# Loads of the next tile in mid-turn of the MLP loop, and a gather ring of 16 slots in the second graph layer

## What is computed

```python
xn = _layernorm(x)
h   = relu(sage_conv(xn, src, dst, W1l, b1, W1r))       # layer 1
gnn = sage_conv(h, src, dst, W2l, b2, W2r)              # layer 2
x = x + gnn + mix(xn)                                   # linear attention, layer norm, MLP, layer norm
x = x + ffn(_layernorm(x))                              # 8 experts, hidden 1024, top 1
# sage_conv: agg = segment_sum(x[src], dst); mean = agg / max(count, 1); mean @ Wl.T + bl + x @ Wr.T
```

## Time and profile before

| what | value |
|---|---|
| time, median of 3 runs | 2454.78 us (2453.99 to 2458.47) |
| the profiled execution: its own time | 2453.61 us |
| its span in the profile | 2451.8 us |
| PE busy | 1925.4 us (79%) |
| DVE busy | 1148.8 us (47%) |
| ACT busy | 549.0 us (22%) |
| POOL busy | 1702.3 us (69%) |
| mean granted clock of PE | 0.891 |

### The profile page before, as it was taken

How to read it: one execution, slowest core, us unless ns; L and a number is a source line. 1 busy time by engine, 2 the same in 40 slices (tenths; PEclk the granted TensorE clock), 3 DMA queues, 4 the chain that set the end, 5 groups by cost and what they waited for, 6 DMA issues and landing times.

```text
span 2451.8 us, 45561 instructions
## 1 busy us (share of the span) xinstructions
PE 1925.4 (79%) x9589; PEld 1190.2 (49%) x9590; DVE 1148.8 (47%) x3201; ACT 549.0 (22%) x1242; POOL 1702.3 (69%) x1773
## 2 busy tenths in 40 slices
PE   3799988878688887776899999877665543679998
PEld 2455555544455555543455555444332211368886
DVE  8544443433577777764555545433332221242221
ACT  6444333333222222221222222111100000101110
POOL 6777777777777777757777777777777777164442
PEclk9999999898899999997899999988776665689999
DMA  7444444444444444434454555444443333245551
GB/s 219 132 124 126 124 123 121 122 118 118 132 135 137 133 133 137 132 97 149 146 166 151 164 157 164 147 153 142 138 141 116 114 116 105 89 141 167 168 167 63
DMA packets 155000, 332.67 MB, mean 136 GB/s; under 512 B 34853, under 2 KB 89095, under 8 KB 154917
## 3 DMA queue, kind: packets, MB, share of 16 engines
q0 software_dynamic: 85824, 248.21, 34.6%
q10 hardware_dynamic: 42630, 58.35, 6.9%
q1 hardware_dynamic: 26466, 25.33, 3.4%
HBM read 273.97 MB, written 58.72 MB: 136 GB/s over the span
## 4 chain that ended last, share of the span: by engine, by line
PE 36%; POOL 33%; issue 15%; DVE 7%; DMA 4%; DVEq 2%; POOLq 2%; ACT 1%; ACTq 1%; SPq 0%
POOL big L699 32%; PE bank L538 12%; PE bank L1728 8%; PE bank L1496 6%; PE bank L1716 2%; PE bank L1502 2%; DMA mbuf<-qT_d 1%; PE bank L1526 1%; PE bank L1651 1%; PE bank L1521 1%; DMA big<-hh_d,edges 1%; POOL big L709 1%; POOLq L696 1%; DMA big<-xh_d,edges 1%; POOLq L694 1%
## 5 line engine op out<-in xcount | busy, mean ns | idle before, releaser
L699 POOL DMA_INDIRECT big<-xh_d,edges x782 | 769.8, 984 | 240.5 <-issue 232.4
L699 POOL DMA_INDIRECT big<-hh_d,edges x782 | 752.4, 962 | 261.1 <-issue 227.2
L1496 PE MATMUL bank<-big,S 128*128 x1960 | 589.0, 427 | 245.8 <-SPq L604 218.4
L898 DVE SCALAR_TENSOR_TENSOR S<-edges,tv,iota 128x512 f16<-128x512 f16 x490 | 368.6, 754 | 450.5 <-PE bank L1496 267.6
L1496 PEld LDWEIGHTS bank<-big,S 128*128 128x128 f16 x1960 | 203.7, 104 | 533.6 <-issue 389.8
L1494 PE MATMUL bank<-ones,S 128*128 128x1 f16 x980 | 165.4, 169 | 73.7 <-SPq L604 63.6
L538 PE MATMUL bank<-turned,x1T 128*128 128x512 f32 x392 | 195.6, 622 | 0.0
L720 POOL DMA_INDIRECT out_dram<-big,node_s x56 | 56.8, 1014 | 145.1 <-DVE big L1231 141.2
L1494 PEld LDWEIGHTS bank<-ones,S 128*128 128x128 f16 x980 | 95.5, 97 | 89.5 <-SPq L604 75.7
L1424 ACT ACTIVATE x1T<-bank 128x256 f32<-128x256 f32 x49 | 18.8, 383 | 531.7 <-PE bank L1502 531.7
L1231 DVE SCALAR_TENSOR_TENSOR big<-bank,prob_s,res 128x256 f32<-128x256 f32 x56 | 27.1, 484 | 179.4 <-PE bank L1730 179.4
(11 more groups left out here) (228 smaller groups left out, 2910.4 us busy)
## 6 DMA issues: line engine op xcount, KB each, us to landing
hx_d<-mbuf ACTq DMA_DIRECT2D x49, 512.0 KB
big<-xh_d,edges POOLq DMA_INDIRECT x782
big<-hh_d,edges POOLq DMA_INDIRECT x782
big<-in_fwd_dram SPq DMA_DIRECT2D x8, 1024.0 KB, 6.4
qT_d<-abuf ACTq DMA_DIRECT2D x49, 128.0 KB
hh_d<-HL ACTq DMA_DIRECT2D x49, 128.0 KB
mbuf<-qT_d ACTq DMA_DIRECT2D x49, 128.0 KB, 2.6
hx_d<-res ACTq DMA_DIRECT2D x49, 128.0 KB
```

Of the source, the lines that this page charges most:

```text
L699: e.indirect_dma_start(G[:, r, n % SC, :], None, table, bass.IndirectOffsetOnAxis(ap=srcx[:, n:n + 1], axis=0)).then_inc(d_g[r], 16)
L898: VI.done(e.scalar_tensor_tensor(S[:, walk.u, :, :], dst[:, bass.ds(c * SC, SC)].unsqueeze(2).to_broadcast([P, SC, P]), tv[:, bass.ds(k, 1 ...
L1496: ins = e.matmul(AGG[:], S[:, walk.u, j, :], G[:, bass.ds(slot, 1), j, :].rearrange("p a c -> p (a c)"), start=False, stop=False, skip_gro ...
```

## The change

Three things are changed.

- In `turn_b` on ACT, `next_loads(i)` stands behind the two `x1T` and ahead of the first `finish1` piece and the Gelus. It was the last thing of the turn.
- In layer 2 the ring has 16 slots instead of eight. They lie from the start of `big`, over `xnT` and half of the old ring. POOL's wait for superchunk c names superchunk c-16. Slots that hold no edges are cleared by two memsets of POOL ahead of the first gather of layer 2, behind a wait for ACT's last read of `xnT`; PE waits for the memsets once.
- Because the new ring lies where the experts' weights go, all eight loads of them are issued by SP behind the last sum of layer 2. The bias `fbd_f` is staged in `late`, and SP's wait for it is gone.

The rest is bookkeeping: the semaphores `d_g` of the eight new slots serve as `d_rb` in the experts' stage, with a base that is added to the counts.

```diff
-RING = 8
+RING, RING2 = 8, 16
+RINGS = RING, RING2
...
+        G2 = big[:, 0:RING2 * SC * C].bitcast(F16).rearrange("p (r j c) -> p r j c", r=RING2, j=SC)
+        GS = G, G2
...
-        fbd_f, fbd_t = big[0:3, 0:NE * C], w2r[0:3].rearrange("p h c -> p (h c)").bitcast(BF16)
+        fbd_f, fbd_t = late[0:3, 0:NE * C], w2r[0:3].rearrange("p h c -> p (h c)").bitcast(BF16)
...
-            EVERY = SUPER // NE // PACK * PACK
-            SOON = XN // (HJ * C)
-
-            def expert_rows(k):
+            for c in range(SUPER):
+                relay(1, c)
+            e.wait_ge(s_sum, NS + 2 * ITEMS)
+            for k in range(NE):
                 e.dma_start(wd[:, k:k + 1, :, :].rearrange("p a j c -> p (a j) c"),
                             w["fwd"][k:k + 1].rearrange("a (j p) c -> p (a j) c", p=P)).then_inc(d_wd, 16)
-            for c in range(SUPER):
-                relay(1, c)
-                k, left = divmod(c + 1, EVERY)
-                if left == 0 and k <= SOON:
-                    if k == 1:
-                        e.wait_ge(s_fbd, 1)
-                    expert_rows(k - 1)
-            e.wait_ge(s_sum, NS + 2 * ITEMS)
-            for k in range(SOON, NE):
-                expert_rows(k)
...
                 else:
+                    AX1.wait(e, "xT", TILES - 1)
+                    for c in range(2):
+                        e.memset(G2[:, ring(1, c), len(chunks(c)):, :].bitcast(F32), 0.0).then_inc(p_setup, 1)
                     e.wait_ge(d_h, 3 * OPENED + 16 * TILES)
...
-                        e.wait_ge(s_sum, held + (c + NS + 1 - RING + layer * ITEMS))
+                        e.wait_ge(s_sum, held + (c + NS + 1 - RINGS[layer] + layer * ITEMS))
...
+                if stage < 2:
+                    next_loads(i)
+                elif stage == 2:
+                    with e.If(i.base < TILES - 1):
+                        next_loads(i)
                 if stage <= 2:
                     walk = Ends(e, raw(i), 1, ITEMS_B, TILES * ITEMS_A)
                     finishes(walk, 1)
...
                 if stage <= 2:
                     finishes(walk, ITEMS_B - 1)
-                if stage < 2:
-                    next_loads(i)
-                elif stage == 2:
-                    with e.If(i.base < TILES - 1):
-                        next_loads(i)
...
-                slot = within(e, walk.c % RING, RING - 1)
+                slot = within(e, walk.c % RINGS[layer], RINGS[layer] - 1)
...
+            e.wait_ge(p_setup, 3 + 8 + 2)
...
-                e.wait_ge(d_rb[u], turn * 16 + 16)
+                e.wait_ge(d_rb[u], turn * 16 + (16 + RB_BASE[u]))
```

More of the change, by code:

```diff
@@ L194, in build @@
         G = ringf.bitcast(F16).rearrange("p (r j c) -> p r j c", r=RING, j=SC)
-        assert XN + (RING - PACK) * SC * C >= WD
+        G2 = big[:, 0:RING2 * SC * C].bitcast(F16).rearrange("p (r j c) -> p r j c", r=RING2, j=SC)
+        GS = G, G2
+        assert XN + (RING - PACK) * SC * C >= max(WD, RING2 * SC * C) and NE * C <= PACK * SC * C
         S = sb("S", [P, NS, SC, P], F16)
@@ L341, in build, with chunks, ring @@
         FR = B7
+        def chunks(c):
+            first = (SUPER - 1 - c) * SC
+            return range(min(first, CHUNKS), min(first + SC, CHUNKS))
+        def ring(layer, c):
+            return (layer * SUPER + 1 + c) % RINGS[layer]
         d_x = [sem(n) for n in ("d_x0_w", "d_x1_w2", "d_x2_wd", "d_x3", "d_x4", "d_x5", "d_x6")]
@@ L346, in build @@
         X_IN = 16 * GROUP
-        d_g = [sem(f"d_g{r}") for r in range(RING)]
+        d_g = [sem(f"d_g{r}") for r in range(RING2)]
         d_edges, d_bias, d_ck, s_gb2, d_fbd = (sem(n) for n in ("d_edges", "d_bias", "d_ck", "s_gb2", "d_fbd"))
@@ L415, in build @@
         s_perm, s_fbd = sem("s_perm"), sem("s_fbd")
-        d_rb = [sem(f"d_rb{u}") for u in range(RB_SLOTS)]
+        assert RING2 - RING == RB_SLOTS
+        d_rb = d_g[RING:]
+        RB_BASE = [16 * sum(len(chunks(c)) for c in range(SUPER) if ring(1, c) == RING + u) for u in range(RB_SLOTS)]
         d_out = [sem(f"d_out{u}") for u in range(OB_SLOTS)]
@@ L539, in matmuls @@
             return ins
-        def chunks(c):
-            first = (SUPER - 1 - c) * SC
-            return range(min(first, CHUNKS), min(first + SC, CHUNKS))
-        def ring(layer, c):
-            return (layer * SUPER + 1 + c) % RING
         def landed(layer, c):
@@ L689, in _ @@
                         e.wait_ge(s_free, 1)
-                    if c >= RING:
-                        n, left = divmod(c - RING, PACK)
+                    if c >= RINGS[layer]:
+                        n, left = divmod(c - RINGS[layer], PACK)
                         if left == 0:
@@ L695, in _ @@
                         held = within(e, (word >> (6 * left)) & 63, TILES - 1)
-                        e.wait_ge(s_sum, held + (c + NS + 1 - RING + layer * ITEMS))
+                        e.wait_ge(s_sum, held + (c + NS + 1 - RINGS[layer] + layer * ITEMS))
                         hold(e)
                     for n in chunks(c):
-                        e.indirect_dma_start(G[:, r, n % SC, :], None, table,
+                        e.indirect_dma_start(GS[layer][:, r, n % SC, :], None, table,
                                              bass.IndirectOffsetOnAxis(ap=srcx[:, n:n + 1], axis=0)).then_inc(d_g[r], 16)
@@ L1495, in add_item @@
                                  skip_group_check=True)
-                    ins = e.matmul(AGG[:], S[:, walk.u, j, :], G[:, bass.ds(slot, 1), j, :].rearrange("p a c -> p (a c)"),
+                    ins = e.matmul(AGG[:], S[:, walk.u, j, :], GS[layer][:, bass.ds(slot, 1), j, :].rearrange("p a c -> p (a c)"),
                                    start=False, stop=False, skip_group_check=True)
```

## The result

The changed kernel took 2467.88 us (median of 7 runs, 2464.72 to 2472.98) against 2458.34 us of the kernel before in the same comparison (7 runs, 2453.99 to 2459.74). The ratio is 1.0043, 95% interval 1.0031 to 1.0055: slower, by 8 to 14 us, where 5.4 us less were forecast. It lies above the range. The profiled executions differ by 14.7 us: 2468.32 against 2453.61 us, with spans of 2466.5 and 2451.8 us.

A forecast was written before the change was run, and what follows sets the result against it. POOL's gathers were taken to bound both layers. Ring -5.4, weights out of layer 2 -0.5 and drain +0.5 gave -5.4 us: 2454.8 to 2449.4 us in medians, with an 8-in-10 range of 2446 to 2456 us.

The forecast's parts named there:

- What bounds the kernel: Both layers: the number of gathers times POOL's 1.25 us sets the time; other engines matter only where POOL waits.
- Loads in mid-turn: MLP loop, layer 1: earlier loads remove most of PE's 64.7 us wait for q; net gain taken as 0.
- the gain of 0 from q's wait: MLP loop: PE's quicker turns gain 0, since layer 1's last gather would start at 1082.3 us all the same.
- The other end: Layer 1, upper bound of loss from ACT's mid-turn wait: 7 turns of 2.8 us less 5.2 absorbed, 14.4 us.
- ACT's wait makes layer 1 slower: Rival, MLP loop: ACT's wait delays `mT` and PE by up to 2.8 us a turn; 2463.8 us, chance 10%.
- place of decision: Layer 1, ahead of superchunk 148: below 1.04 us a turn over five turns, POOL's ring absorbs the delay.
- The ring of 16: Layer 2: POOL runs 8 superchunks further ahead, so its four pauses go; gain 5.4 us.
- The memsets: Between the layers: POOL's two clears and their wait are covered by its wait for `hh_d`; cost 0.
- Weights out of layer 2: Layer 2: six 1 MB loads no longer run beside gathers; gain 0 to 1.8 us, taken as 0.5.
- Weights behind the last sum: After layer 2: eight weight loads stay hidden before the experts' first transpose, by 6 to 43 us.
- The drain's 0.5 us: Last tiles after layer 2: Gelus may wait for stores slowed by weight loads; bounds 0 and 4.1 us, 0.5 taken.
- The rival of the blocked stores: After layer 2: stores must let all queued weights pass, +16 us, 2465 us; chance 4%.

The follow-up runs named there:

- the waits alone: Kernel before with ACT's two waits (DVE's `s`, PE's `t`) moved to mid-turn, both loads still issued at the turn's end: 1.0053 of the kernel before at 2457.7 us.

## Why the prediction was wrong

*What bounds the kernel.* Right: POOL's gathers set both layers, and both effects of the change on them are pauses of POOL, gone or new.

*Loads in mid-turn.* Here it failed, in the choice between two ends of a range that was itself too short. The mechanism was written down, with its 2.8 us in seven turns, and the gain of 0 from q's wait was right. The step that failed is "I take 0, since DVE is the late one and needs none of this before its next turn". DVE does need it within the turn: its one-hots of the next item go into the slots of `S` that PE's sum frees, and that sum stands behind `mT` in PE's queue (4.67 us of waiting at 744.24). It hides little, then: with two slots of `S` in use in this loop PE's delay becomes DVE's in the same turn. The other end, 7 x 2.8 less 5.2 = 14.4 us, is near what the waits alone cost (12.8 us, or 2.8 us a turn), but by luck: the 2.8 us was meant to hold the loads too, and no lower clock. Against the changed kernel it lacked two things. I had counted the loads as 0.87 us, from start to end of their rows; `mT` came 1.16 us later through them, and later in 10.0 us of the layer with what follows. And PE's lower clock after the longer wait was not in the sum at all: 2.8 us more of matmul time in the turn that is shown, some 1.3 of which the turn got longer by. The two turns with a tile's end in the second item were left out too (1.75 us each).

*The rival* "ACT's wait makes layer 1 slower" is what happened, from the point that it named (1.04 us a turn). It had 10% and 2463.8 us. For its place of decision it spoke of five turns ahead of superchunk 148. The trace has four of the seven there, and both of those with an end in the second item. And POOL pauses already at superchunk 130, and behind 148 up to 1001 us, so seven or nine turns count.

*The ring of 16.* Right in place: the pauses are gone. Right in size for the execution that it was read from: 5.4 us between two kernels on one chip, 5.4 forecast. In other executions with a ring of 8 the pauses held up to 10.1 us, so the gain has a range that the forecast didn't give.

*The memsets.* Right: 8.2 us of waiting are left behind them.

*Weights out of layer 2.* 0.5 us forecast, nothing to be seen above a spread of 5 us.

*Weights behind the last sum.* Right: hidden, by 43 us, the upper end of my 6 to 43. The eight loads took some 30 us, as the 31 of the forecast; 354 to 373 GB/s is what they moved together with the stores. The drain's 0.5 us was some 0.1 for the one Gelu that named a store, and the whole stretch to the experts was 0.7 us shorter. The Trainium skill (DMA: Bandwidth & Descriptors, Queues, rings and completion order) says that each DMA engine takes turns between its queues by packets; the trace agrees, since a store issued among 8 MB of loads landed within 6.4 us, and not at 2151 us with them. The rival of the blocked stores falls.

*What was in no term*: 7.0 us behind the last instruction of PE. With ring only, which is the change without the mid-turn loads, the ratio 0.9943 is 14 us (the medians are 15.9 apart). 7.0 are this and 5 to 10 the ring. So with the loads in mid-turn costing nothing, as forecast, the forecast would still have been some 9 us too high.

*Numbers*: faster had 50%, slower 12%. The chance for slower hung on one argument about DVE's queue that I had not followed in the timeline: DVE's next one-hot stands a few rows below `s` and names what it needs.

## What to carry to other kernels

Before a wait is moved up an in-order queue, list what is queued behind it up to its old place, and for each of these what its consumer has queued behind it in turn, within the same turn and not the next. Here one piece of work, with `mT` first in it, made the difference between 23 us lost and nothing. A wait that goes on an engine which doesn't set the pace is worth nothing, so the move should risk nothing either: put the loads behind the last operation that someone waits for. And where an engine is the late one by a full buffer, its depth says how much delay it can take: compare that with the sum over all turns.

## What the runs showed of the hardware

- The granted clock of TensorE went to its lower level behind single waits of 2.2 to 4.6 us in the MLP loop, and the group of four matmuls behind such a wait then took 1.6 to 1.9 us instead of 1.03. In the turn shown this was 2.8 us more of matmul time and some 1.3 us more of the turn. In the kernel before it happened in 2 of 9 tile ends. What decides it in a given turn the runs don't show: with the waits alone one tile end had its matmuls at full speed behind a wait of 2.8 us.
- Two loads issued by ACT cost the operation behind them 1.16 us (2.18 less 1.02), while their own rows are 0.34 us each.
- While 8 MB of loads issued by SP in a row were under way, the DMA engines moved 354 to 373 GB/s, ACT's stores included. The Gelu that waited for one of these stores came 6.4 us after its issue, where it came 6.2 us after it without most of the loads.
- Behind the last instruction that the profile shows, the same program end lasts 2.5 or 9.5 us (from POOL's last scatter), the same in every profile of a given kernel, on every chip. The cause is open.
- The kernel before takes 2458 us on some chips and 3138 to 3214 us on others. There PE stands still for up to 13.7 us with nothing named that it waits for, its mean granted clock is 0.79 to 0.80 instead of 0.88 to 0.89, and POOL is no longer the bound of layer 1. An edit that takes away 5 us of POOL's pauses isn't seen there at all.
